# First stage reordered on three engines, and four hidden tiles of the experts made in the drain of the attention loop

## The reference

```python
# tokens: embedding and a window mean of 20 features, fused, layer norm
fused = concat(emb[ids], window3(pca[ids]) @ proj_w + proj_b) @ fus_w + fus_b
h = layernorm(fused) * ln_g + ln_b
# attention: 16 heads of 64, width 256, on the layer norm of h
q, k, v = xWq + bq, xWk + bk, xWv + bv
y = x + softmax(q k / 8) v Wo + bo ;  h = h + layernorm(y)
# 16 experts of 64: each of 128 positions' top 2 (over the 32 rows), each expert takes
# the best 64 positions of 128 per row; gelu(x w1 + b1) w2 + b2, added where taken
h = h + layernorm(x + sum over experts) * gamma + beta
```

## Time and profile before

| | |
|---|---|
| median of 3 runs | 570.81 us (569.54 to 571.08) |
| profiled execution | 572.44 us; its span on the core 570.7 us |
| busy: PE, PEld | 526.0 us (92%), 395.0 us (69%) |
| busy: DVE, ACT, POOL | 453.3 us (79%), 357.1 us (63%), 387.5 us (68%) |
| first block | 0 to 66.7 us; PE busy 48.5, DVE 44.3, ACT 22.7 |
| attention loop | 66.7 to 386.6 us; PE busy 303.4 of 319.9 |
| hidden tiles and routing | 386.6 to 424.4 us |
| second expert layer | 424.4 to 552.9 us, and the last four sequences |
| mean granted TensorE clock | 0.963 |

### The profile page before, as it was taken

One profiled execution on the slowest core, in us unless ns is written; L12 is line 12 of the kernel. 1 busy time (PEld: TensorE's weight loads), 2 busy tenths in 40 slices (PEclk: granted clock), 3 DMA queues, 4 the chain that ended last, 5 costly groups with the idle time before them and its releaser, 6 DMA issues. The chain is left out here.

```text
span 570.7 us, 16170 instructions
## 1 busy us (share of the span) xinstructions
PE 526.0 (92%) x6063; PEld 395.0 (69%) x6063; DVE 453.3 (79%) x1019; ACT 357.1 (63%) x744; POOL 387.5 (68%) x512
## 2 busy tenths in 40 slices
PE   4797788999999999999999999839999999999985
PEld 2697666778777777777777777624457777777774
DVE  5785466889888888888888888977846888887776
ACT  1215767788787877878778787614584655565540
POOL 3050235888787877878778787942095977898783
PEclk9957799999999999999999999987999999999998
DMA  6800000000000000000000000000633044053011
GB/s 208 325 2 1 2 1 2 4 3 2 3 3 3 2 3 3 3 3 3 4 3 2 4 3 3 2 0 2 151 85 83 20 110 102 22 141 85 24 45 55
DMA packets 11905, 21.73 MB, mean 38 GB/s; under 512 B 4668, under 2 KB 9780, under 8 KB 10164
## 3 DMA queue, kind: packets, MB, share of 16 engines
q1 hardware_dynamic: 11828, 20.71, 13.1%
HBM read 16.24 MB, written 4.33 MB: 36 GB/s over the span
## 5 line engine op out<-in xcount | busy, mean ns | idle before, releaser
L768 POOL TENSOR_TENSOR s_pl<-s_pf,s_ph 128x512 f16<-128x512 f32 x128 | 147.0, 1160 | 15.3 <-ACT s_ph L860 15.3
L949 DVE TENSOR_REDUCE s_mx<-ps 128x4 f32<-128x512 f32 x128 | 83.8, 677 | 29.1 <-PE ps L1090 29.1
L1503 PE MATMUL ps<-s_xt_all,s_w1s 128*128 128x512 f16 x384 | 89.9, 387 | 0.8 <-PEq L751 0.8
L1526 PE MATMUL ps<-s_w2s,s_hid 128*128 128x256 f16 x768 | 88.9, 273 | 0.0
L854 ACT ACTIVATE s_pf<-ps 128x512 f32<-128x512 f32 x128 | 76.6, 602 | 16.9 <-PE ps L1103 16.9
L1526 PEld LDWEIGHTS ps<-s_w2s,s_hid 128*128 128x128 f16 x768 | 75.1, 98 | 11.1
L860 ACT ACTIVATE s_ph<-s_pf 128x512 f16<-128x512 f32 x128 | 77.2, 637 | 0.0
L1136 PE MATMUL ps<-s_zh,s_cth 128*128 128x256 f16 x256 | 69.8, 273 | 0.0
L1136 PE MATMUL ps<-s_zl,s_cth 128*128 128x256 f16 x256 | 69.8, 273 | 0.0
L1136 PE MATMUL ps<-s_zh,s_ctl 128*128 128x256 f16 x256 | 69.8, 273 | 0.0
L1503 PEld LDWEIGHTS ps<-s_xt_all,s_w1s 128*128 128x128 f16 x384 | 38.1, 100 | 42.4 <-issue 4.5
(11 more groups left out here) (230 smaller groups left out, 1252.3 us busy)
## 6 DMA issues: line engine op xcount, KB each, us to landing
s_rep<-picks SPq DMA_DIRECT2D x14, 512.0 KB, 6.6
s_stage<-in_w SPq DMA_DIRECT2D x2, 1024.0 KB, 13.9
out<-s_ot_a SPq DMA_DIRECT2D x16, 128.0 KB, 1.7
out<-s_lg SPq DMA_DIRECT2D x16, 128.0 KB, 1.7
s_stage<-in_wq SPq DMA_DIRECT2D x1, 1024.0 KB, 4.7
s_stage<-in_wk SPq DMA_DIRECT2D x1, 1024.0 KB, 6.4
s_stage<-in_wv SPq DMA_DIRECT2D x1, 1024.0 KB, 8.1
s_stage<-in_wo SPq DMA_DIRECT2D x1, 1024.0 KB, 9.9
```

The costliest lines, as they stand in the source:

```text
L768: nc.gpsimd.tensor_tensor(flat(pl[:, b % 2, 4 * j:4 * j + 4, :]), pf[:, j, :], flat(ph[:, b % 2, 4 * j:4 * j + 4, :]), ALU.subtract).then_ ...
L949: nc.vector.tensor_reduce(mx[:, b % 2, c:c + 4], A[ab][:].rearrange("p (h k) -> p h k", h=4), AX.X, ALU.max).then_inc(max_done[hf][ab], 1)
L1503: mm = nc.tensor.matmul(HB[j % NH][:], w1s[:, wp, c, j * P:(j + 1) * P], xt_all[:, GB * g:GB * (g + 1), xp, c, :], start=(k == 0), stop=(k ...
L1526: mm = nc.tensor.matmul(zb[b % 4], hid[:, g % 2, hp, j, t * P:(t + 1) * P], w2s[:, wp, j, :], start=False, stop=(j == NJ - 1 and hp == 1))
```

## The change

1. `centre_wo` moves from VectorE to ScalarE, as eight sums with an accumulator output (each waits for the one before), one scaled copy and eight additions of 256 elements; it comes ahead of the roots in ScalarE's list.
2. The copies of tables 0 to 2 (`table`) move from VectorE to ScalarE: table 0 between the sums and the additions, table 1 between the two square roots, table 2 behind the load of the Exp table.
3. TensorE's list: 12 fillers, quads 0 and 1, table 0, quads 2 and 3, tables 1 and 2. The fillers before quads 2 and 3 go; those before `u_cols` are 6, not 8.
4. In the u phase VectorE copies the fourth bank of each octet and its low parts come in another order; ScalarE copies three banks, and its list is reordered.
5. Hidden tiles 0 to 3 of group 0 are made in the second block, one in step 30 and three in step 31. `hidden_beside` gives 4 tiles beside sequence 0 (2 before) and runs two tiles ahead from then on. `routes` comes behind tile 9.
6. Low parts 6 and 7 of group 0 are made by VectorE. ScalarE's first `hi` comes behind the fifth Gelu of group 2.

```diff
         nc.scalar.activation(mr[0:UD, :], mbo[:], ACT.Copy, scale=Y_SCALE).then_inc(mr_ok, 1)
 
-        for n, (v, root) in enumerate(((v1, q1), (v2, q2))):
+        def root(n, v, r):
             act.wait_ge(v_ok, n + 1)
-            nc.scalar.activation(root[:], v[:], ACT.Sqrt).then_inc(sqrt_ok, 1)
+            nc.scalar.activation(r[:], v[:], ACT.Sqrt).then_inc(sqrt_ok, 1)
+
+        def table(n):
+            act.wait_ge(in_w[n], 32)
+            act.wait_ge(qkv_ready, n + 1)
+            nc.scalar.activation(qkv_t[:, n], TABLE_BANKS[n][:].rearrange("p (c u) -> p c u", c=HD), ACT.Copy).then_inc(qkv_ok, 1)
+            act.wait_ge(qkv_ok, 2 * n + 1)
+            nc.scalar.activation(qkv_t[:, n, :, ONE:ONE + 1], bT[:, n, :].rearrange("p (c o) -> p c o", o=1), ACT.Copy)\
+                .then_inc(qkv_ok, 1)
+
+        act.wait_ge(in_wo, 16)
+        for c in range(HD):
+            nc.scalar.activation(wo_sum[:], wo_v[:, c, :], ACT.Identity, accum_out=wsum[:, 0, c:c + 1]).then_inc(wo_step, 1)
+            act.wait_ge(wo_step, c + 1)
+        nc.scalar.activation(wsum[:, 1, :], wsum[:, 0, :], ACT.Copy, scale=-1.0 / D).then_inc(wo_step, 1)
+        act.wait_ge(wo_step, HD + 1)
+        table(0)
+        for c in range(HD):
+            nc.scalar.activation(wo_v[:, c, :], wo_v[:, c, :], ACT.Identity, bias=wsum[:, 1, c:c + 1]).then_inc(wo_step, 1)
+        root(0, v1, q1)
+        table(1)
+        root(1, v2, q2)
         nc.scalar.preload_act_table(ACT.Exp)
+        table(2)
 
...
         u_hi(0)
         u_hi(1)
-        for n in range(4):
+        u_hi(2)
+        for n in range(3):
             u_cols(0, n)
+        u_hi(3)
         g_hi()
-        u_hi(2)
-        for n in range(4):
-            u_cols(1, n)
-        u_hi(3)
-        for n in range(4):
-            u_cols(2, n)
-        for n in range(4):
+        for g in (1, 2):
+            for n in range(3):
+                u_cols(g, n)
+        z_hi(0)
+        z_hi(1)
+        for n in range(3):
             u_cols(3, n)
-        for n in range(4):
-            z_hi(n)
+        z_hi(2)
+        z_hi(3)
...
             then(nc.vector.scalar_tensor_tensor(out=sig[:], in0=v2[:], scalar=1.0 / T_SCALE, in1=r2[:], op0=ALU.mult, op1=ALU.mult))
 
+        def u_cols(g):
+            dve.wait_ge(ut_ready, 4 * g + 4)
+            nc.vector.tensor_copy(ub_b[:, 4 * g + 3, :], UT_BANKS[3][:]).then_inc(ut_last_ok, 1)
+
         def u_rows(g):
             s = octet(g)
             dve.wait_ge(cleared, CLEARED["uf"])
             nc.vector.tensor_tensor(uf[:, s, 0:2 * V], nb[:, s, 0:2 * V], bcast(r12[:, s], 2 * V), ALU.mult).then_inc(uf_ok, 1)
             nc.vector.tensor_copy(uf[:, s, R2:R2 + 1], r2[:, s].rearrange("p (b o) -> p b o", o=1)).then_inc(uf_ok, 1)
+
+        def u_lo(g):
+            s = octet(g)
+            dve.wait_ge(uf_ok, 2 * g + 2)
             dve.wait_ge(uh_ok, g + 1)
...
                 .then_inc(zlo_ok, 1)
 
-        def centre_wo():
-            dve.wait_ge(in_wo, 16)
-            nc.vector.reduce_sum(wsum[:, 0, :], wo_v, AX.X).then_inc(wo_step, 1)
...
-            dve.wait_ge(wo_step, 2)
-            nc.vector.tensor_tensor(wo_v, wo_v, bcast(wsum[:, 1, :], D), ALU.add).then_inc(wo_step, 1)
-
-        centre_wo()
-        table(0)
         for g in range(NQ):
             quads(g)
         roots()
         u_rows(0)
-        table(1)
         u_rows(1)
-        table(2)
+        u_lo(0)
+        u_rows(2)
+        u_lo(1)
+        u_cols(0)
+        u_rows(3)
+        u_lo(2)
         g_lo()
-        u_rows(2)
-        u_rows(3)
+        u_lo(3)
+        for g in range(1, NQ):
+            u_cols(g)
         for n in range(4):
             z_lo(n)
 
...
                 pe.wait_ge(prod_ok, 2 * NQ)
             for n in range(4):
-                if g >= 1:
-                    pe.wait_ge(ut_ok, 4 * g - 3 + n)
+                if g >= 1 and n < 3:
+                    pe.wait_ge(ut_ok, 3 * g - 2 + n)
+                elif g >= 1:
+                    pe.wait_ge(ut_last_ok, g)
                 for k in range(2):
                     for a, src in ((0, uh), (1, ul)):
                         x = (2 * k + a) * P
...
             mm.then_inc(z_ready, 1)
 
+        keep_going(12, psum[0][:, 0:FREE])
+        quads(0)
+        quads(1)
         table(0)
-        for g in range(NQ):
-            if g >= 2:
-                keep_going(8, psum[0][:, 0:FREE])
-            quads(g)
+        quads(2)
+        quads(3)
         table(1)
         table(2)
         keep_going(8, psum[0][:, 0:FREE])
         u_cols(0)
         gram()
         for g in range(1, NQ):
-            keep_going(8, psum[5][:, 0:FREE])
+            keep_going(6, psum[5][:, 0:FREE])
             u_cols(g)
         for n in range(4):
...
+h_ready = sem("h_ready")
+
+def hidden_tile(g, j):
+    k = 0
+    for c in range(KC):
+        for wp, xp in ((0, 0), (0, 1), (1, 0)):
+            mm = nc.tensor.matmul(HB[j % NH][:], w1s[:, wp, c, j * P:(j + 1) * P],
+                                  xt_all[:, GB * g:GB * (g + 1), xp, c, :], start=(k == 0), stop=(k == 5))
+            k += 1
+    mm.then_inc(h_ready, 1)
 
 with nc.Block() as block:
     @block.sync
...
                 token_rows(n)
 
+        def first_hidden(j):
+            if j < 2:
+                pe.wait_ge(max_done[1][j], B)
+            else:
+                pe.wait_ge(exp_done[j], B)
+            pe.wait_ge(xlo_done, GB)
+            hidden_tile(0, j)
+
         BETWEEN = {(-4, 0): 10, (-4, 1): 6, (-3, 0): 10, (-3, 3): 6, (-2, 0): 10, (-2, 2): 8}
 
         for i in STEPS:
...
+            if i == B - 2:
+                first_hidden(0)
+            if i == B - 1:
+                for j in (1, 2, 3):
+                    first_hidden(j)
             if has(i):
                 x_cols(i)
...
 
 def hidden_beside(b):
-    first, last = (min((n * 40 + 25) // 26, NJ * (NG - LEAD)) for n in (b, b + 1))
+    first, last = (min((n * 40 + 25) // 26 + 2, NJ * (NG - LEAD)) if n else 0 for n in (b, b + 1))
     return [(LEAD + k // NJ, k % NJ) for k in range(first, last)]
 
 def masks_beside(b):
     q = b + PAIRS
     return [(q // 4, 2 * (q % 4) + n) for n in range(2)] if q < 4 * NG else []
+
+def lo_by_dve(g, j):
+    return g == 0 and j >= 6
+
+def lo_count(g, j):
+    return min(j + 1, 6) if g == 0 else NJ * g + j - 1
 
 FIRST_MASKS = [(q // 4, 2 * (q % 4) + n) for q in range(PAIRS) for n in range(2)]
...
             if g == 2 and j == 0:
                 act.wait_ge(gate, gate_steps[0])
-            if g >= 3:
-                act.wait_ge(glo_done, NJ * (g - 3) + j + 1)
+            if g >= 3 and lo_by_dve(g - 3, j):
+                act.wait_ge(glo_front, j - 5)
+            elif g >= 3:
+                act.wait_ge(glo_done, lo_count(g - 3, j))
             nc.scalar.activation(gelu_tile(g, j), HB[j % NH][:], ACT.Gelu, bias=b1T[:, j:j + 1], scale=1.0 / W_SCALE)\
                 .then_inc(gelu_done, 1)
...
                 gelu(g, j)
         for j in range(NJ):
+            if j >= 5:
+                hi(*FIRST_MASKS[j - 5])
             gelu(LEAD - 1, j)
-            hi(*FIRST_MASKS[j])
-        for g, j in FIRST_MASKS[NJ:]:
+        for g, j in FIRST_MASKS[NJ - 5:]:
             hi(g, j)
         for b in range(B):
...
                     round_of(n, r)
                 choose(n)
-        for g, j in FIRST_MASKS:
+        for g, j in FIRST_MASKS[:NJ]:
+            masked(g, j)
+        for j in (6, 7):
+            dve.wait_ge(ghi_done, j + 1)
+            nc.vector.tensor_tensor(hid[:, 0, 1, j, :], gelu_tile(0, j), hid[:, 0, 0, j, :], ALU.subtract).then_inc(glo_front, 1)
+        for g, j in FIRST_MASKS[NJ:]:
             masked(g, j)
         for b in range(B):
...
             g, t = b // GB, b % GB
             if t == 0:
-                pe.wait_ge(glo_done, NJ * (g + 1))
+                pe.wait_ge(glo_done, lo_count(g, NJ - 1))
+            if b == 0:
+                pe.wait_ge(glo_front, 2)
             if b % 8 == 0:
                 pe.wait_ge(takes_in, 16 * 4 * (b // 8 + 1))
...
             mm.then_inc(z_ready4, 1)
 
-        for g in range(LEAD):
-            for j in range(NJ):
-                hidden(g, j)
-                if (g, j) == (0, 3):
-                    routes()
+        for n in range(NH, NJ * LEAD):
+            hidden(n // NJ, n % NJ)
+            if n == 9:
+                routes()
         for b in range(B):
             for g, j in hidden_beside(b):
                 hidden(g, j)
```

More of the change, by code:

```diff
@@ L182, in build @@
         root_count = [0]
-        uf_ok, uh_ok, ul_ok, ut_ready, ut_ok = (sem(n) for n in ("uf_ok", "uh_ok", "ul_ok", "ut_ready", "ut_ok"))
+        uf_ok, uh_ok, ul_ok, ut_ready, ut_ok, ut_last_ok = (sem(n) for n in ("uf_ok", "uh_ok", "ul_ok", "ut_ready", "ut_ok", "ut_last_ok"))
         qkv_ready, qkv_ok, g_ready, ghi_ok, glo_ok, z_ready, zhi_ok, zlo_ok, wo_step = (
@@ L611, in z_part @@
                     if n == 0:
-                        pe.wait_ge(wo_step, 3)
```

(22 more changed lines are left out.)

12 lines of the change are left out of this document (1 added, 11 removed).

## The result

The changed kernel takes 568.88 us (median of 20 runs, 566.4 to 571.27) where the kernel before took 570.76 (20 runs, 569.28 to 572.25): a ratio of 0.9971, 95% interval 0.9959 to 0.9983. It is faster, by 1.9 us (1.7 by the ratio); forecast were 6.2, and the time lies outside the range of 560.8 to 567.3. The profiled execution took 570.79 us, 1.9 above its median, with a span of 569.0 against 570.7 before (also 1.7 above its median). So the profiles show 1.7 us of gain.

The account below looks back on a forecast made before the run. Four successive stretches bound the kernel, VectorE's queue being the first stage's long wait; the second expert layer's start sets the end. First stage 5.7 plus drain 0.5 gave 6.2 us: 570.81 to 564.6, range 560.8 to 567.3.

Parts of the forecast that it names:

- The roots: First stage, up to the roots: first step issued 4.8 us earlier, but GpSimd's hold leaves only 0.8 us saved.
- Rival A: First stage: the port does not hold small operations, roots save 4.0 us more, end 560.6; chance 0.12.
- rival B: First stage: first root step loses the race, u phase hand-offs cost 0.2 us more each, end about 567.3; chance 0.15.
- the race: Roots: whether the first step slips in at 33.1 between two GpSimd split operations; if lost, nothing of the 4.8 us kept.
- up to three times: Centring's additions moved to ScalarE: the Trainium skill's figure for how much faster VectorE does additions.
- The u phase: First stage after the roots: 14.25 us of VectorE work plus 4.85 of waits, 19.1 us; 4.9 saved by fewer waits.
- the ring: u phase: TensorE finishes columns of g + 1 only after VectorE's copy of g; waits 0.35 and 1.0 us.
- What is saved before it should arrive at the end whole: Loop over 32 sequences: without outside input after the first stage, it passes on that stage's whole saving, 5.7 us.
- The drain: Loop's end and third block: four tiles moved into TensorE's waits, second layer from 423.9, gain 0.5 us.
- rival C: Third block: route transposes come 5.5 us later, a rigid chain delays the second layer up to 8.5, end 573.6; chance 0.05.
- the slack that I had named: Third block, argument against rival C: ScalarE had the first mask waiting nearly 4 us before it took it.
- The tail: After the second layer's start: two fewer tiles, at sequences 24 and 25, give nothing, as GpSimd sets the pace there.

Follow-up runs that it names:

- the late split: The changed kernel with GpSimd's split of the first-layer weights moved to the loop's opening: 565.29 us, 5.3 below the kernel before.
- the four profiles of this first stage: Profiles of the changed kernel, the first stage alone, the change with routes behind tile 6, and the warm drain: u phase 21.34, 21.51, 19.91, 19.91 us.
- the drain alone: The kernel before with only the change's drain and third block, its first stage left as it was: 572.66 us, 1.8 above the kernel before.
- the first stage alone: The kernel before with only the change's first stage, its drain, third block and masks left as they were: 568.75 us, 3.3 below before.
- the warm drain: The changed kernel with spare TensorE products in the drain's two waits and at the third block's head: 566.41 us, 5.0 below before.
- the fastest kernel: The changed kernel with later split, routes behind tile 6, spare products in first stage, drain and third block, last first-stage group 14: 559.22 us.

## Why the prediction was wrong

**The roots: right, and a little better.** First step at 32 forecast, 32.06 measured; slipped in between two operations of GpSimd; the next held to 37.3 forecast, 37.07 measured. The u phase began at 40.80, forecast 41.6, so the roots saved 1.6, not 0.8. Rival A is excluded by the change's own profile, and the late split shows the size of the hold: a root chain 3.9 us shorter, 3.6 in the times. What rival B adds is small: where the race was lost, the last root step came 4.5 us after GpSimd's end (37.84 to 42.32), where it was won 3.55 (37.02 to 40.57). ScalarE was through with the centring at 30.65, forecast 30.9. Its eight additions took 3.29 us, VectorE's one had taken 2.29: a factor of 1.4. The prediction's "up to three times" is a figure for bf16, and these are fp32.

**The u phase: the mechanism right, the term mis-sized.** From its first row to the last low part of z it took 21.34 us (40.80 to 62.14) where it had taken 24.05: saved 2.7, not 4.9. Its work is as forecast (14.2 us). Its waits are 7.1 us (0.58 + 0.41 + 1.29 + 0.49 + 1.34 + 1.85 + 1.16 in VectorE's timeline), not 4.85. I gave TensorE a half clock for the first column products only, and let it recover for good. It fell a second time, behind the waits of the ring that I had worked out myself, and z took 3.05 us in place of 2.01. That fall comes in some executions only: in two of the four profiles of this first stage it is missing, the waits are 5.7 us and the phase takes 19.91, which saves 4.1. So 1.4 of the missing 2.2 us are this second fall, and 0.8 are waits priced too low even without it.

**"What is saved before it should arrive at the end whole": this step failed.** The loop has no input from outside, but it has a clock that it inherits. In the profile before it opened half warm: its first product at 66.77, half clock from 67.8 to 71.2. Window of the kernel before, columns as above:

```profile
67.80:71.20 3.40, 3.40 (x19) 2.40 (x17) 2.15 (x4) 2.38 (x6) 3.08 (x4) 0.50 0.05 8
```

In the changed one half clock reigned from 61.4 to 68.1. The loop's first 5.65 us ran at it, 2.25 more than before, which took 1.1 us back. The tiles in the drain did not (the drain alone shows that). Of the four profiles of this first stage three open the loop cold (321.6 to 322.1 us up to the table's load) and one, the first stage alone, does not (319.9). Spare products ended it: 2.8 us for this and z together.

**The drain: "gain 0.5, bounds +1.7 and -1.0" failed**, in sign and in what ends last. TensorE's part was right (first tile at 386.59; table load at 384.56 and the forecast's 1.28 + 0.69 give 386.5; "it will be cold again": 3.05 us over, 2.8 forecast). But I took the second layer to start when TensorE's order let it, with masks and low parts undisturbed: 423.9, which is 36.2 us after the table's load. Measured are 38.2. Of these 2.0 us, 0.7 come from my taking the early end of my own range, for six low parts from 416.1 end at 424.6. Another 0.5 are GpSimd's start, 28.9 us after the load and not 28.4. The last 0.75 is a term that I had put at nothing: masks and low parts met, and six low parts took 9.27 us in place of 8.53.

The routes came, as rival C had it, behind six cold tiles: 12.7 us after the table's load, not 6.9. The chain behind them was rigid as far as the masks, which came 26.2 us after the load, not 20.4: the same 5.8. There the slack that I had named absorbed most of it, and what was left made masks and low parts meet. I knew the hold and had applied it to the roots, yet not to the third block. C had 0.05. As a mechanism it was at work, at a small part of its price: the whole drain lost 1.5 to 1.8 us, not 8.5, and the routes' place is about 1.0 of it (1.4 by the times). The larger lever is the clock, 2.6 us in this stretch and 3.3 in the times when held warm.

**The tail: right.** Its two fewer tiles gave nothing (146.3 us from the second layer to the end before, 146.2 after).

**Why the range missed.** The clock was priced at the first column products and in the third block. It hangs as well at the end of the u phase (1.4 us, in some executions) and at the loop's opening (1.1). The range had room for hand-offs, not for a colder loop, and it took a shift of the routes to be harmless short of rival C. Its upper end was rival B's 567.3; B's own terms give 567.0 (570.8 - 3.3 - 0.5), which changes nothing here.

## What to carry to other kernels

When a stage becomes shorter by taking waits out of one engine, list which engine's long operations stand beside its short ones at the new time, and do so again for every later stage whose chains shift. Where TensorE waits, look at the granted clock of the stage behind the wait, not only at that of the wait; a handful of spare products there can be worth more than the reordering (here 2.8 and 3.3 us by the times, against 1.7 of the whole change), as long as they end before the others do. Where the profile names an engine as the one waited for, look when that engine was done: here in seven of the kernels it was done over 0.6 us before the wait ended, and another ended last. Before a size is read from one profile, look whether a second one of the same code shows it: the second fall of the clock was there in two of four. A move that is right by itself can hide a loss in the same diff: time the halves.

## What was not expected of the hardware

- A VectorE operation on 32 elements took 4.07 us (0.18 without GpSimd at work) with one source from SBUF, and 3.42 us (0.19) with two. In each of these rows GpSimd's operation had started first. In the profile with the warm drain VectorE's first root step started at 31.21, GpSimd's operation at 31.52, and the step took 0.26. The reciprocal on 32 elements was not held in any of four profiles where it ran beside GpSimd (0.35 us, as without it).
- Operations of like length take turns: masks of 512 columns took 1.65 us each beside GpSimd's subtractions (0.69 alone), the subtractions 1.60 (1.16 alone), and both engines started one every 1.57 us.
- The runs of one kernel differ by their clock. Of the changed kernel's 20, the ten with a mean granted clock of 0.979 and up took 566.4 to 568.97 us, the ten below it 567.98 to 571.27. In the fastest kernel three runs at 0.998 took 558.06 to 559.22 and two at 0.994 and 0.995 took 561.27 and 561.5; the profile of one of these has one cold stretch, early in the loop (74 to 80 us). Why it comes in some runs only stays open.
- The load of the Gelu table took 1.28 us and the first Gelu followed 0.01 us behind it. ScalarE's sums with an accumulator read took 0.54 us per 256 elements, the wait on itself included; 0.55 was forecast.
